# Decoder block with routed experts on Trainium2: row gathers issued one tile earlier, and a new order of instructions where the shared experts end and at the last expert tile

## The reference

```python
h = _rms(x, w_ln2).reshape(B * S, H)                     # 2048 tokens of 512
probs = softmax(h @ w_router)                            # 8 experts
top_w, top_i = top_k(probs, 2)
g = einsum('th,ehi->eti', h, w_gate_e)                   # 352 wide per expert
u = einsum('th,ehi->eti', h, w_up_e)
y = einsum('eti,eih->eth', silu(g) * u, w_down_e)
routed = einsum('eth,te->th', y, combine)                # weights of the two chosen experts
sh = silu(h @ w_sh_gate) * (h @ w_sh_up) @ w_sh_down     # shared experts, 1408 wide
x = x + routed + sh * sigmoid(h @ w_sh_eg)
```

## Time and profile before

| what | value |
|---|---|
| time, median of 3 runs | 2153.02 us (2152.26 to 2156.55) |
| the profiled execution's own time | 2159.8 us |
| its span in the profile | 2158.0 us |
| PE busy | 1987.8 us, 92% |
| DVE, ACT, POOL busy | 63%, 49%, 33% |
| granted TensorE clock, mean | 0.963 |

### The profile page before, as it was taken

The page is one execution under the profiler, slowest core; times in us unless marked ns, Lnnn a source line. Parts: engine busy times, 40 slices in busy tenths (PEclk is TensorE's granted clock), DMA queues, the critical chain, the costliest instruction groups (busy, mean ns, idle before and its releaser), DMA issues. The chain is left out here.

```text
span 2158.0 us, 32705 instructions
## 1 busy us (share of the span) xinstructions
PE 1987.8 (92%) x10991; PEld 1385.7 (64%) x10991; DVE 1356.9 (63%) x2805; ACT 1048.9 (49%) x1890; POOL 701.9 (33%) x610
## 2 busy tenths in 40 slices
PE   7998999968799999997988899979999999899998
PEld 6875666656533433344877566657788888777775
DVE  6455566557799798985787566645223244677675
ACT  3424454445378676764543445534222121566664
POOL 0003655436513232322665565521000000233333
PEclk9998899989899999998999799999999999999999
DMA  5637676247664545435475767545021126433332
GB/s 200 223 145 179 139 170 154 87 166 273 238 168 118 139 119 147 107 99 150 171 234 200 159 155 170 124 135 214 1 98 45 34 88 244 127 64 63 67 69 38
DMA packets 151994, 297.75 MB, mean 138 GB/s; under 512 B 24722, under 2 KB 43284, under 8 KB 150740
## 3 DMA queue, kind: packets, MB, share of 16 engines
q1 hardware_dynamic: 114052, 242.29, 37.9%
q10 hardware_dynamic: 29040, 34.74, 6.0%
q0 software_dynamic: 8736, 18.62, 4.7%
HBM read 181.55 MB, written 102.50 MB: 132 GB/s over the span
## 5 line engine op out<-in xcount | busy, mean ns | idle before, releaser
L1339 ACT ACTIVATE cross_c_prob<-bank 128x512 f32<-128x512 f32 x512 | 271.1, 598 | 114.4 <-PE bank L1192 113.0
L1389 DVE TENSOR_REDUCE row_max<-bank 128x2 f32<-128x1024 f32 x248 | 290.7, 1212 | 24.9 <-PE bank L1158 23.9
L1856 PE MATMUL bank<-moe_hT,moe_w 128*128 128x512 f32 x1056 | 249.7, 392 | 9.6 <-DVE moe_w L2129 9.6
L1192 PE MATMUL bank<-stack 56*128 56x512 f32 (+4 forms) x768 | 231.5, 425 | 6.1 <-ACT cross_c_prob L1339 3.1
L1856 PEld LDWEIGHTS bank<-moe_hT,moe_w 128*128 128x128 f32 x1056 | 198.8, 189 | 51.8 <-issue 9.8
L1158 PE MATMUL bank<-stack 48*128 48x512 f32 (+4 forms) x720 | 191.3, 443 | 26.5 <-PEq L71 13.7
L1192 PEld LDWEIGHTS bank<-stack 56*128 56x128 f32 (+1 forms) x768 | 118.1, 192 | 134.3 <-ACT cross_c_prob L1339 69.3
L1339 ACT ACTIVATE rotary_c_prob<-bank 128x512 f32<-128x512 f32 (+3 forms) x256 | 105.8, 436 | 124.5 <-PE bank L1195 121.7
L1339 ACT ACTIVATE first_c_prob<-bank 128x512 f32<-128x512 f32 (+3 forms) x256 | 105.9, 436 | 123.6 <-PE bank L1195 121.3
L1385 DVE CUSTOM_DVE_ANT_0 first_c_masked<-bank,later 128x128 f32<-128x128 f32 (+3 forms) x240 | 109.0, 486 | 80.8 <-PE bank L1158 80.0
L1158 PEld LDWEIGHTS bank<-stack 48*128 48x128 f32 (+1 forms) x720 | 93.4, 196 | 100.4 <-DVE row_max L1389 46.2
(11 more groups left out here) (402 smaller groups left out, 4482.3 us busy)
## 6 DMA issues: line engine op xcount, KB each, us to landing
qk_parts<-first_p_parts SPq DMA_DIRECT2D x32, 512.0 KB, 2.7
stack<-qk_parts SPq DMA_DIRECT2D x64, 256.0 KB, 6.4
qk_parts<-cross_p_parts SPq DMA_DIRECT2D x32, 512.0 KB, 2.6
stack<-qk_parts SPq DMA_DIRECT2D x256, 64.0 KB, 2.5
qk_parts<-rotary_p_parts SPq DMA_DIRECT2D x32, 512.0 KB, 2.8
moe_gate_up_e<-in_experts_gate_up SPq DMA_DIRECT2D x8, 1408.0 KB, 8.9
moe_raw<-in_shared_packed SPq DMA_DIRECT2D x11, 768.0 KB, 8.4
stack<-qk_parts SPq DMA_DIRECT2D x16, 512.0 KB, 5.4
```

Source lines behind the costliest of these rows:

```text
L1192: last = nc.tensor.matmul(bank[:, 0 : S - q0], k_stack[slot][r : r + ALL_ROWS, at, m * P : (m + 1) * P], q_stack[slot][r : r + ALL_ROWS, a ...
L1339: nc.scalar.activation(probability(g, step // HEADS_AT_ONCE, step % HEADS_AT_ONCE), psum[bank_at["score", n]][:, 0 : S - q0], ACT.Exp).the ...
L1389: nc.vector.tensor_reduce(row_max[:, g % 2, m, j - 1 : j + 1], c.banks[:, first : first + WIDE, :], AX_X, ALU.max).then_inc(s.max_done, 1)
L1856: last = nc.tensor.matmul(psum[bank][:], weights(pa, f, k), hT[p % 2][:, pb, k, :], start=m == 0, stop=m == len(steps) - 1)
```

## The change: what it does

- **Gathers.** POOL's loop becomes: gather(t + 4), wait for result(t), scatter(t). The wait for the last plain store of `out` (`s_stored`) moves behind the fifth gather, right ahead of scatter 0.
- **First tiles.** front(0) stands ahead of the last `down`. Chunks 0 and 1 both lie outside the shared weights (`chunks01`, over `x3_tile` among others, so ACT waits for the last residual sum first), and both are made ahead of columns_high(0). The evacuation of the last batch is no longer one piece: its four instructions stand one by one among the splits of tiles 0 and 1. gate_up(1) waits for two of them, and is cut in two halves with turn(0) between; down_e(0) and down_e(1) wait for the third and the fourth. down_e(0) follows gate_up(1) as before.
- **Last tile.** down_e(37) stands after gate_up(38) as before, but turn(38) is put ahead of its third matmul, which needs one more load of the owner.

The diff, cut to its core:

```diff
+        with ExitStack() as after_routing:
+            chunks01 = after_routing.enter_context(nc.sbuf_tensor("moe_chunks01", [P, 2, 2, CHUNK], F32R))
+        x3_tile = sb("x3_tile", [P, D])
...
-        w_chunk = (chunk0[:], chunks12[:, 0], chunks12[:, 1], chunk3)
+        w_chunk = (chunks01[:, 0], chunks01[:, 1], chunk2[:], chunk3)
...
-                pool.wait_ge(s.s_stored, 16 * B)
                 for t in range(PER):
+                    if t + 4 < PER:
+                        gather(t + 4)
                     pool.wait_ge(s.e_result, t + 1)
                     if t:
                         pool.wait_ge(s.e_added, 16 * t)
+                    else:
+                        pool.wait_ge(s.s_stored, 16 * B)
                     pool.indirect_dma_start(a.out, bass.IndirectOffsetOnAxis(ap=token[:, t : t + 1], axis=0), y[:, t % 2, :], None,
                                             bounds_check=B * S - 1, oob_is_err=False, compute_op=ALU.add).then_inc(s.e_added, 16)
-                    if t + 4 < PER:
-                        gather(t + 4)
...
-                down(N_F - 1)
...
-                def gate_up(t):
-                    pe.wait_ge(s.e_hT_lo, t + 1)
-                    if t == 1:
-                        pe.wait_ge(s.s_out, TT * B)
-                    if t >= 2:
-                        pe.wait_ge(s.e_inner, t - 1)
-                    for k in range(KD):
+                def gate_up(t, pieces):
+                    if 0 in pieces:
+                        pe.wait_ge(s.e_hT_lo, t + 1)
+                        if t == 1:
+                            pe.wait_ge(s.s_out, TT * LAST + 2)
+                        if t >= 2:
+                            pe.wait_ge(s.e_inner, t - 1)
+                    for k in pieces:
...
+                def down_e(t, pieces):
+                    if 0 in pieces:
+                        pe.wait_ge(s.e_innerT, t + 1)
+                        pe.wait_ge(s.e_innerT01, t + 1)
+                        if t == 0:
+                            pe.wait_ge(s.e_down_here, 16 * E)
+                        if t < 2:
+                            pe.wait_ge(s.s_out, TT * LAST + 3 + t)
+                        else:
+                            pe.wait_ge(s.e_result, t - 1)
...
+                down(N_F - 1)
+                front(1)
+                gate_up(0, range(KD))
+                front(2)
+                gate_up(1, (0, 1))
+                turn(0)
+                gate_up(1, (2, 3))
+                down_e(0, range(3))
+                for t in range(2, PER):
                     if t + 1 < PER:
                         front(t + 1)
-                    if t:
-                        turn(t - 1)
-                    gate_up(t)
-                    if t:
-                        down_e(t - 1)
+                    turn(t - 1)
+                    gate_up(t, range(KD))
+                    if t + 1 < PER:
+                        down_e(t - 1, range(3))
+                down_e(PER - 2, (0, 1))
                 turn(PER - 1)
-                down_e(PER - 1)
+                down_e(PER - 2, (2,))
+                down_e(PER - 1, range(3))
...
-                    elif k:
+                    elif k >= 2:
...
+                act.wait_ge(s.s_residual, TT * B)
                 act.wait_ge(s.e_gate_up_here, 16 * E)
                 e = owner_of(0)
                 chunk_high(0, 0, e)
+                chunk_high(0, 1, e)
                 columns_high(0)
-                for k in range(1, KD):
-                    chunk_high(0, k, e)
+                chunk_high(0, 2, e)
+                chunk_high(0, 3, e)
...
+                chunk_low(0, 1, e)
                 columns_low(0)
-                for k in range(1, KD):
-                    chunk_low(0, k, e)
-                evacuate(LAST)
-                for t in range(PER):
-                    if t:
-                        turned_inner(t - 1)
+                evacuate(LAST, (0,))
+                chunk_low(0, 2, e)
+                chunk_low(0, 3, e)
+                e = owner_of(1)
+                columns_low(1)
+                evacuate(LAST, (1,))
+                chunk_low(1, 0, e)
+                chunk_low(1, 1, e)
+                multiply(0)
+                evacuate(LAST, (2,))
+                chunk_low(1, 2, e)
+                evacuate(LAST, (3,))
+                chunk_low(1, 3, e)
+                for t in range(1, PER):
+                    turned_inner(t - 1)
```

More of the change, by code:

```diff
@@ L1690, in moe_phase @@
             rt, squares = sb1("rt", [n_col, S]), sb1("squares", [P, D])
-        with ExitStack() as after_routing:
-            chunk0 = after_routing.enter_context(nc.sbuf_tensor("moe_chunk0", [P, 2, CHUNK], F32R))
         nmax, ex, total = sb("nmax", [P, NT]), sb("ex", [P, NT, E]), sb("total", [P, NT])
@@ L1715, in moe_phase @@
         gate_up_e, down_w_e = sb("gate_up_e", [P, E, GATE_UP_W]), sb("down_w_e", [P, E, DOWN_W])
-        chunks12 = sb("chunks12", [P, 2, 2, CHUNK], F32R)
-        sb("w_pad", [P, SHARED_W * 2 - 4 * CHUNK])
+        chunk2 = sb("chunk2", [P, 2, CHUNK], F32R)
+        sb("w_pad", [P, SHARED_W * 2 - 2 * CHUNK])
         hT_e, silu_e, inner_e = sb("hT_e", [P, 2, 2, KD, P], F32R), sb("silu_e", [P, 2, FE]), sb("inner_e", [P, 2, FE])
@@ L1959, in down_e @@
                     e = pe.value_load(owner[0:1, t : t + 1], min_val=0, max_val=E - 1)
-                    for n, (k0, kn) in enumerate(FE_K):
+                    for n in pieces:
+                        kn = FE_K[n][1]
                         rhs = w_dn_e[0:kn, bass.ds(e, 1), n, :].rearrange("p a n -> p (a n)")
                         last = nc.tensor.matmul(psum[6 + t % 2][:], innerT[0:kn, t % 2, n, :], rhs, start=n == 0, stop=n == len(FE_K) - 1)
-                    last.then_inc(s.e_down, 1)
+                        if n == len(FE_K) - 1:
+                            last.then_inc(s.e_down, 1)
@@ L2141, in make_gate, with evacuate @@
                     nc.vector.reciprocal(gate[:, tiles], gate[:, tiles]).then_inc(s.m_gate, 1)
-                def evacuate(p):
-                    dve.wait_ge(s.s_down, KF * (p + 1))
-                    dve.wait_ge(s.s_residual, TT * (p + 1))
-                    dve.wait_ge(s.m_gate, p + 1)
-                    for t in range(TT):
+                def evacuate(p, tiles):
+                    if 0 in tiles:
+                        dve.wait_ge(s.s_down, KF * (p + 1))
+                        dve.wait_ge(s.s_residual, TT * (p + 1))
+                        dve.wait_ge(s.m_gate, p + 1)
+                    for t in tiles:
                         n = p * TT + t
@@ L2256, in _ @@
                         if f == 0 and p:
-                            evacuate(p - 1)
+                            evacuate(p - 1, range(TT))
                         if p < LAST:
@@ L2305, in turned_inner, with multiply @@
                     nc.vector.tensor_copy(innerT[0:kn, t % 2, 2], psum[Y][0:kn, 2 * P : 3 * P]).then_inc(s.e_innerT, 1)
+                def multiply(t):
+                    dve.wait_ge(s.e_silu, t + 1)
+                    if t >= 2:
+                        dve.wait_ge(s.e_inner_turned, t - 1)
+                    nc.vector.tensor_tensor(inner_e[:, t % 2], silu_e[:, t % 2], psum[2 + 2 * (t % 2)][:, 0:FE], ALU.mult).then_inc(s.e_inner, 1)
                 dve.wait_ge(s.m_owners, 4)
@@ L2321, in _ @@
                             chunk_low(t + 1, k, e)
[L2322 to L2325 removed]
+                    multiply(t)
                     if t + 1 < PER:
```

6 lines of the change are left out of this document (1 added, 5 removed).

## The result

| | before | changed |
|---|---|---|
| median of 6 runs, us | 2154.47 (2147.78 to 2158.53) | 2133.37 (2128.70 to 2141.35) |
| ratio, 95% interval | | 0.9909 (0.9883 to 0.9934) |
| span of the profiled execution, us | 2158.0 | 2132.7 |

The changed kernel is 0.91% faster, 21.1 us by the medians; the interval reaches from 14 to 25 us. Timed once more later, beside other runs of the kernel before, it had 0.9888 (0.9864 to 0.9912). Forecast were 23.8 us less and 2129.2 us.

A forecast was written before the change was run, and what follows sets the result against it. PE, busy for 92% of the span, was taken as the bound, so only its waits or slow work could be won: 17.9 + 5.0 + 0.9 = 23.8 us, from the median 2153.0 to 2129.2; range 2126 to 2138.

The forecast's parts named there:

- rival A: Whole program: the forecast itself holds, 2126 to 2133 us; chance 0.75.
- rival C: Head: the new order gives nothing and the clock falls; 18.8 us won in all, 2134; chance 0.09.
- The gathers: Turn(1) to turn(36): no gather late any more, 35 tiles at 7.20 us, 252.0 in place of 269.91, 17.9 won.
- The bound of 6.3 us: Routed tiles: a scatter lands within 6.3 us, so a tile of 7.20 leaves room for it.
- The hand-over: From shared to routed part: turn(1) at 1859.4 and not 1863.90; 4.5 to 5.5 us won, taken as 5.0.
- The clock: Hand-over: full clock throughout; if it fell once to 1.2 GHz, the head would be worth 3.5 us.
- The covers: Start of the routed part: fifth gather, last store of out and residual sums cost nothing; the store's cover is 0.4 us.
- The last tile: End: turn(38) ahead of down_e(37)'s third part wins 0.9 us, or 0 if the landing of the scatter before holds it.
- B: Middle: another wait takes part of the steady gain, a tile takes 7.45 us; 2138 in all; chance 0.09.
- D: Middle: the gathers do not limit, their wait returns under another name; 5.9 us won in all, 2147; chance 0.03.
- E: Middle: scatters land too late and set the tile; landing 7.05 us cancels the gain, 7.3 gives 2162; chance 0.03.
- without effect: Whole program: the change has no effect on the time; chance 0.01.

The follow-up runs named there:

- The early load: The changed kernel with PE's owner loads for down_e(0), down_e(37) and down_e(38) moved ahead: head 19.73 us, tail 16.60, ratio 0.9876 to the kernel before.
- one piece: The changed kernel with the last batch's four evacuations in one piece again, ahead of chunk 2 of tile 0: head 19.72 us, middle 251.54, no timed ratio.
- The two runs that keep the old head: The kernel before with gather(t + 4) ahead of the wait for result(t) (ratio 0.9925), or between that wait and scatter(t) (0.9931).
- swapping two lines: The kernel before with gather(t + 4) issued between the wait for result(t) and scatter(t): middle 252.23 us, ratio 0.9931.

## Why the prediction was right, step by step

- **The total.** The changed kernel stands at 2133.4 us, inside the range of 2126 to 2138, but 0.4 above what rival A named and 0.6 below the 2134 of rival C. The gain by the medians, 21.1, is 2.7 short of the forecast, where the routed part has 23.45 against 23.8. Single executions of the changed kernel lie between 2128.7 and 2141.4, so where the median falls within a few us is chance, and the total by itself can't tell A from C. The stretches can.
- **The gathers, 17.9 forecast.** Right in mechanism: from a gather that lands 7.8 us behind the end of down_e against a tile of 7.2. Done alone it measured 17.7, and in the changed kernel 18.3. That differences of start times give the size, and not the 12.6 us that the profile lists as idle, is shown by the same numbers.
- **The Trainium skill's price of a transfer** (DMA: Bandwidth & Descriptors, Anatomy of one DMA), an estimate of 2.6 us for such a gather, would have led to no gain in the middle. The runs have 4.3 behind a scatter and 3.4 ahead of one, so neither agrees with it.
- **What would be late next.** Nothing was: the middle of the changed kernel has no idle PE, DVE and ACT are busy for 191 and 177 of 251 us. The bound of 6.3 us on the landing of a scatter held: 4.8 by the median, 5.3 at most.
- **The hand-over, 5.0 forecast (4.5 to 5.5), 4.34 measured.** The slip is in the step from DVE's last copy to down_e(0). I took 0.87 us for the load, as at the end of the kernel before, where PE had nothing left to do but wait for the copy. Here PE's queue was held at a chunk until shortly before, and the step took 1.70. That is the term that was mis-sized, by 0.83. The early load takes that away and measures 5.5 in all. That "DVE ends last" was right: from its first evacuation at the end of the last down to its last copy are 9.9 us (1843.01 to 1852.92), against the sum of 10.3 less the overlap. That DVE's order would not matter was not claimed in the prediction but by me later, and fell: the order that the change chose costs 1.15 us against one piece.
- **The clock, no fall forecast.** Right: 1.00 throughout, with three waits of 0.2 to 0.5 us and the one for the owner. In the kernel before, PE stood still for 2.30 us ahead of turn(0), and from 1855 to 1858 it had half of the clock, its lower level of 1.2 GHz. Turn(0) and gate_up(1) in the chain of before, then a gate_up in the middle of the changed kernel:

```profile
1855.32 0.90 PE bank L1949 x3
1856.22 4.82 PE bank L1939 x24
```

```profile
1865.44 3.84 PE bank L1942 x24
```

  Of the 4.34 us some 1.4 are thus the clock, an estimate: 4.82 against 3.84, and a turn of 0.90 against 0.49. The two runs that keep the old head have 5.95 and 5.96 for this turn and gate_up together, where before has 5.72, which accounts for their head of 25.4 and not 25.2. No run took the clock alone.
- **The covers.** The fifth gather, the store of out (4.3 us), and the residual sums cost nothing, as said, and the cover of the store was better than the 0.4 us forecast. The store was issued at 1851.56 and took 4.3, so it was there by 1855.9, 1.6 ahead of result(0) at 1857.50.
- **The last tile, 0.9 forecast, 0.77 measured, 0.71 by the run that undid it.** The bound that was named, the landing of scatter 37, is just reached: result ready at 2127.51, landed 2.7 behind 2124.85, at 2127.5.
- **6.8 us between the profiled execution and the median.** I put them outside the routed part. The two profiles of the changed kernel bear this out: spans of 2132.7 and 2138.2, and the same stretches to 0.07.

The rivals fell: B (a tile of 7.45) by 7.19, C (no gain in the head) by 4.3 us there and a clock that stayed up, D (the wait comes back) by the gathers alone, E (landing) by the landing itself, at most 5.3 us against 7.05, and "without effect" by the ratio.

## What to carry to other kernels

A buffer that is refilled behind another instruction of the same queue is late by that instruction's whole round. Add up the round from the trace and set it against the time of a tile: once it is below, more lead brings nothing, and here swapping two lines brought the same as a tile of lead. A load of a register ahead of matmuls cost nothing in the middle, where PE never waited, and over a microsecond where PE had just been held, so put it ahead of the last wait and not behind it. To spread a block of work among waiting work is no gain in itself; move only the part that nobody waits for, and read the stretch, since a timing of the whole could not see 1 to 2 us here.

## What the runs showed of the hardware that was not expected

- The same gather, 256 KB in 128 rows, landed in 3.4 us (3.2 to 4.0) when issued ahead of a scatter and in 4.3 (3.3 to 5.3) right behind one. It started 0.26 us behind the end of the ACT result that POOL was waiting for; a scatter in the same place took 0.82 by the median of all 39 (0.77 to 0.94 in the kernel before).
- The scatters of the last tiles, beside which the DMA queues moved 0 GB/s (2110.5 to 2132.7 in the changed kernel), landed in 2.7 us each. By the median of all 39 a scatter took 4.8, at most 5.8 in any run here.
- With a load of the owner in between, down_e started 0.87 us behind the copy that PE was waiting for. Where PE had been held at a chunk until 0.5 us before that copy ended, it started 1.70 behind the copy and 0.95 behind the last matmul. Loaded early it showed no idle time, and none in the middle, where every tile has such a load.
- Without late gathers the tile is 7.19 us in all kernels with the changed placement of chunks and 7.21 in the two that had the placement of before (252.24 and 252.23 against 251.5 to 251.6 for 35 tiles). It is 0.7 us in the whole; where it comes from stays open.
- Over the 13 profiled executions the start of the head lay between 1826.6 and 1842.3 us, in kernels whose instructions are the same up to there, while head, middle and tail of the changed kernel, profiled twice, repeated to 0.07 us. So the time of the whole program varies ahead of the routed part, by about as much as the executions of one kernel differ. From the first use of `hT` in the shared part to the head all 13 took 388.9 to 390.4 us. From the first to the last use of the attention probabilities they took 238.0 to 246.7 in the first layer, 238.2 to 246.8 in the third and 397.5 to 400.9 in the second, so most of the spread lies in the two causal layers. What varies there stays open.
